# 14 dense blocks in place of 13, 23 gathered groups in place of 25, and earlier loads and verdict around the hand-over, in a graph network of two layers

## The reference, cut to what matters

```python
def _L0_gnn_ref(h, W, src, dst):      # three hops over the normalised graph
    x = h
    for _ in range(3):
        msg = (x * norm_out[:, None])[src]
        agg = segment_sum(msg, dst)
        x = 0.5 * (agg * norm_in[:, None]) + 0.5 * h
    return x @ W.T

def _L1_gnn_ref(x, edge_index, W1, b1, W2, b2, gamma, beta):
    edge_feat = concatenate([x[src], x[tgt]], axis=1)
    w = sigmoid(relu(edge_feat @ W1 + b1) @ W2 + b2)[:, 0]
    agg = segment_sum(w[:, None] * x[src], tgt)
    return layernorm(x + agg) * gamma + beta

x = layernorm(x + _L0_gnn_ref(x, ...))
x = layernorm(x + _L1_gnn_ref(x, ...))
```

## Time and profile before

| | us |
|---|---|
| median of three runs | 1170.32 (1169.7 to 1171.43) |
| the profiled execution's own time | 1174.88 |
| its span, first to last instruction | 1173.1 |
| TensorE busy | 955.8 |
| VectorE busy | 984.7 |
| ScalarE busy | 608.5 |
| POOL busy | 602.5 |

### The profile page before, as it was taken

One profiled execution on the slowest core, in us unless ns is written; L12 is line 12 of the kernel. 1 busy time (PEld: TensorE's weight loads), 2 busy tenths in 40 slices (PEclk: granted clock), 3 DMA queues, 4 the chain that ended last, 5 costly groups with the idle time before them and its releaser, 6 DMA issues.

```text
span 1173.1 us, 33827 instructions
## 1 busy us (share of the span) xinstructions
PE 955.8 (81%) x11293; PEld 789.2 (67%) x11294; DVE 984.7 (84%) x2684; ACT 608.5 (52%) x1511; POOL 602.5 (51%) x745
## 2 busy tenths in 40 slices
PE   3666666668888998989947999999999998899960
PEld 2666666657667887777825777888777777677750
DVE  7988888879999999777637999999898888788866
ACT  7555555541110000122236878788777777677765
POOL 2000000024676444466577677777777777777711
PEclk8999999979988999999968999999999999999975
DMA  3000000000000000011147677777766776676601
GB/s 98 1 0 0 0 0 0 1 1 2 2 2 3 3 3 3 20 35 43 49 128 218 194 211 217 218 213 217 222 200 207 204 209 199 191 222 198 200 15 56
DMA packets 77515, 117.43 MB, mean 100 GB/s; under 512 B 20488, under 2 KB 38972, under 8 KB 77372
## 3 DMA queue, kind: packets, MB, share of 16 engines
q1 hardware_dynamic: 58172, 63.13, 18.0%
q0 software_dynamic: 19200, 52.45, 15.9%
HBM read 108.66 MB, written 6.86 MB: 98 GB/s over the span
## 4 chain that ended last, share of the span: by engine, by line
DVE 32%; PE 26%; POOL 21%; issue 13%; ACT 4%; DMA 2%; SPq 1%; DVEq 1%; POOLq 0%; ACTq 0%
POOL region L937 13%; PE bank L1795 6%; DVE stage L1043 5%; POOL U L937 5%; PE bank L1680 5%; DVE aggT L1226 2%; PE bank L1682 2%; DVE stage L1206 2%; DVE stage L1219 2%; PE bank L1892 2%; POOL stage L937 2%; DVE aggT L1043 2%; PE bank L1917 1%; PE bank L1904 1%; PE bank L1756 1%
## 5 line engine op out<-in xcount | busy, mean ns | idle before, releaser
L937 POOL DMA_INDIRECT region<-src_split,region x272 | 265.0, 974 | 86.3 <-issue 81.5
L1795 PE MATMUL bank<-U,region 128*128 128x256 f16 (+1 forms) x1875 | 244.2, 282 | 6.6 <-DVE U L1310 3.8
L1795 PEld LDWEIGHTS bank<-U,region 128*128 128x128 fp8e4 x1875 | 184.0, 101 | 43.0 <-DVE U L1310 4.3
L2181 ACT CAST region<-bank 128x512 f16<-128x512 f32 x338 | 180.7, 591 | 0.0
L2059 ACT CAST region<-bank 128x500 f32 x202 | 119.9, 594 | 92.1 <-PE bank L1682 68.1
L2161 ACT ACTIVATE region<-bank 128x512 f16<-128x512 f32 x169 | 100.9, 597 | 63.9 <-PE bank L1895 58.3
L1680 PE MATMUL bank<-stage 128*128 128x175 f16 x544 | 92.1, 254 | 49.1 <-DVE aggT L1043 25.8
L1467 DVE SCALAR_TENSOR_TENSOR region<-bank,region 128x512 f16<-128x512 f32 x169 | 116.4, 689 | 12.8 <-ACT region L2161 9.9
L826 POOL TENSOR_TENSOR aggT<-stage 128x520 f16<-128x520 f16 x52 | 76.2, 1485 | 93.7 <-DVE stage L1203 84.1
L1892 PE MATMUL bank<-region,xs 128*128 128x256 f16 x676 | 104.2, 278 | 20.8 <-DVE region L1467 13.5
L1451 DVE TENSOR_SCALAR region<-region,stage 128x512 f16<-128x512 f16 x338 | 109.6, 366 | 12.5 <-DMA region<-slot_rows 12.5
(11 more groups left out here) (292 smaller groups left out, 2350.8 us busy)
## 6 DMA issues: line engine op xcount, KB each, us to landing
region<-slot_rows SPq DMA_DIRECT2D x169, 256.0 KB
region<-in_dst_dram SPq DMA_DIRECT2D x100, 64.0 KB
region<-src_split,region POOLq DMA_INDIRECT x272
slot_rows<-aggT SPq DMA_DIRECT2D x104, 3.2 KB
src_split<-U SPq DMA_DIRECT2D x25, 64.0 KB, 1.6
src_split<-xs SPq DMA_DIRECT2D x25, 64.0 KB, 1.5
tgt_split<-q SPq DMA_DIRECT2D x25, 64.0 KB, 1.6
region<-tgt_split SPq DMA_DIRECT2D x100, 16.0 KB
```

Of the source, the lines that this page charges most:

```text
L937: nc.gpsimd.indirect_dma_start(out=rows_of(n, i), out_offset=None, in_=src_split, in_offset=bass.IndirectOffsetOnAxis(ap=listed[n % LISTS] ...
L1795: z = nc.tensor.matmul(bank[2 * (k % 2) + p][:, 0:width], count[:, h, b * P:(b + 1) * P], U[k % 2][:, h, 0:width], start=h == 0, stop=h == ...
L2181: nc.scalar.copy(y_rows[u % 4][:, a, :], bank[3 + a][:, :]).then_inc(rows_copied, 1)
```

## The change

- `FIRST_BLOCK` goes from 12 to 11 and `POOLED` from 25 to 23: 14 dense blocks with 14 x 13 = 182 units and 28 half-blocks to sort, and 92 batches. The loop has 188 steps; the batches lie on steps 12 to 183.
- `targets_of` and `load_slots` stand further up in SP's program, and a new `first_loads` asks for list 0, the first targets and lists 1 and 2 ahead of the last `tables`. It waits for the end of the hops, the table of block 11 and the stored lists.
- `window` becomes `window_half`: two of a group's four batches per call, four DMAs, in two neighbouring batch steps; the first two windows come in steps 2 to 5, each half after a list.
- VectorE no longer waits for `pq_split` ahead of the loop, and TensorE waits in each unit of the first dense block for the two source blocks that it reads.
- `judge_landed` stands ahead of the loop, its product on TensorE after step 6 and in bank 2, `raise_flag` in step 8; TensorE's wait for the flag stands at the first `sums`.
- `qwin` and the last block of `turned_slots` have SBUF of their own.

```diff
-    POOLED = 25
+    POOLED = 23
-    FIRST_BLOCK = 12
+    FIRST_BLOCK = 11
...
-        qwin = [carve(region, taken, [2 * D], f16) for _ in range(2)]
+        qwin = [sb(f"qwin{i}", [P, 2 * D], f16) for i in range(2)]
...
-        turned_slots = [carve(aggT, taken, [P], f16) for _ in range(DENSE)]
+        turned_slots = [carve(aggT, taken, [P], f16) for _ in range(DENSE - 1)]
+        turned_slots.append(sb("turned_last", [P, P], f16))
...
+            def first_loads():
+                sp.wait_ge(hop_psum, 3 * NB)
+                sp.wait_ge(q_tabled[FIRST_BLOCK % 2], 16 * (FIRST_BLOCK // 2 + 1))
+                sp.wait_ge(slots_stored, 64 * HALF_BLOCKS)
+                load_slots(0)
+                targets_of(0)
+                load_slots(1)
+                load_slots(2)
...
             for c in range(NB + 2):
+                if c == NB + 1:
+                    first_loads()
                 tables(c, c % 2)
...
-            sp.wait_ge(hop_psum, 3 * NB)
-
-            def window(n, p):
-                if n >= 2:
-                    sp.wait_ge(ohT_ready, n - 1)
-                    sp.wait_ge(s_psum, (n - 1) * BPS)
-                first = load_four(ET.SP, base[0], n, N)
-                for q in range(BPS):
-                    sp.dma_start(qwin[p][q * QR:(q + 1) * QR, :], tgt_split[bass.ds(first[q], QR), :])\
+            window_first = [None]
+
+            def window_half(n, p, half):
+                if half == 0:
+                    if n >= 2:
+                        sp.wait_ge(ohT_ready, n - 1)
+                        sp.wait_ge(s_psum, (n - 1) * BPS)
+                    window_first[0] = load_four(ET.SP, base[0], n, N)
+                for q in range(half * BPS // 2, (half + 1) * BPS // 2):
+                    sp.dma_start(qwin[p][q * QR:(q + 1) * QR, :], tgt_split[bass.ds(window_first[0][q], QR), :])\
                       .then_inc(win_loaded[p], 16)
-                for q in range(BPS):
                     at = n * (BPS * BE) + q * BE
...
-            targets_of(0)
-            sp.wait_ge(slots_stored, 64 * HALF_BLOCKS)
-            load_slots(0)
+
             for s in range(STEPS):
                 b = batch_at[s]
-                if s + 1 < TOTAL:
+                if 2 < s + 1 < TOTAL:
                     load_slots(s + 1)
-                if s == 1:
-                    window(0, 0)
-                    window(1, 1)
-                if b is not None and b % BPS == 0 and 2 <= b // BPS + 1 < POOLED:
-                    window(b // BPS + 1, (b // BPS + 1) % 2)
+                if 2 <= s < 6:
+                    window_half((s - 2) // 2, (s - 2) // 2, s % 2)
+                if b is not None and b % BPS < 2 and 2 <= b // BPS + 1 < POOLED:
+                    window_half(b // BPS + 1, (b // BPS + 1) % 2, b % BPS)
...
-            dve.wait_ge(pq_split, NB)
             dve.wait_ge(slots_ready, HALF_BLOCKS)
...
-                if s == 0:
-                    judge_landed()
-                if s == 4:
+                if s == 8:
                     raise_flag()
...
+            judge_landed()
             first = None
             for s in range(STEPS):
...
                 pe.wait_ge(ohw_ready, b + 1)
+                if b == 0:
+                    pe.wait_ge(flag_ready, 1)
...
                 pe.wait_ge(turned_ready, u + 1)
+                if at == 0:
+                    latest = max(source_block(u, 0), source_block(u, 1))
+                    pe.wait_ge(y_split, latest + 1)
+                    pe.wait_ge(pq_split, latest + 1)
                 if u % UNITS == 0:
-                    pe.wait_ge(y_split, NB)
-                    pe.wait_ge(pq_split, NB)
                     pe.wait_ge(q_loaded[at % 2], 32 * (at // 2 + 1))
...
-                    if u == 3:
-                        pe.wait_ge(flag_ready, 1)
                     sum_pair(u - 3)
...
-                if s == 2:
+                if s == 6:
                     pe.wait_ge(chain["verdict"], 7)
-                    nc.tensor.matmul(bank[7][0:1, 0:3], one[:, :], verdict_sums[:, :], start=True, stop=True)\
+                    nc.tensor.matmul(bank[2][0:1, 0:3], one[:, :], verdict_sums[:, :], start=True, stop=True)\
```

More of the change, by code:

```diff
@@ L635, in _, with targets_of, load_slots @@
               .then_inc(w_loaded, 16)
+            def targets_of(i):
+                here = (FIRST_BLOCK + i) * P
+                if i >= 2:
+                    sp.wait_ge(pair_psum, (i - 1) * UNITS)
+                for half in range(2):
+                    sp.dma_start(q_pair[i % 2][half * HD:(half + 1) * HD, :, :],
+                                 tgt_split[here:here + P, half * D:(half + 1) * D]
+                                 .rearrange("(a r) k -> r a k", a=2)).then_inc(q_loaded[i % 2], 16)
+            def load_slots(u):
+                i, m = divmod(u, UNITS)
+                if u >= 3:
+                    sp.wait_ge(turned_ready, u - 2)
+                sp.dma_start(slots_here[u % 3][:, :], slot_rows[i, m:m + 1, :].broadcast_to([P, 8 * P]))\
+                  .then_inc(slots_loaded[u % 3], 16)
+            def first_loads():
[6 more added lines that the diff above has]
+                load_slots(2)
             def store_slots(hs):
@@ L1547, in raise_flag @@
                 dve.wait_ge(verdict_psum, 1)
-                nc.vector.tensor_copy(flag_f[:, 0:1], bank[7][0:1, 0:1])
-                nc.vector.tensor_scalar(flag_f[:, 1:2], bank[7][0:1, 1:2], float(E), None, ALU.not_equal)
-                link(nc.vector.tensor_scalar(flag_f[:, 2:3], bank[7][0:1, 2:3], 0.0, None, ALU.not_equal))
+                nc.vector.tensor_copy(flag_f[:, 0:1], bank[2][0:1, 0:1])
+                nc.vector.tensor_scalar(flag_f[:, 1:2], bank[2][0:1, 1:2], float(E), None, ALU.not_equal)
+                link(nc.vector.tensor_scalar(flag_f[:, 2:3], bank[2][0:1, 2:3], 0.0, None, ALU.not_equal))
                 link(nc.vector.tensor_tensor(flag_f[:, 0:1], flag_f[:, 0:1], flag_f[:, 1:2], ALU.add))
```

14 lines of the change are left out of this document (removed).

## The result

The changed kernel takes **1194.0 us** (median, 1190.56 to 1195.39), the kernel before in the same comparison 1170.41: 23.6 us slower by the medians. The ratio over all executions is 1.0189, interval 1.0171 to 1.0207, some 22 us. The prediction said 1169.8 with a range of 1159 to 1178. The profiled execution took 1194.06 us, its span is 1192.2 (1173.1 before).

The account below looks back on a forecast made before the run. POOL's gathers were taken to bound the loop's last 288 us, the engines' unit steps the part before. Terms -1.0 + 10.5 - 5.2 - 4.8 = -0.5 us took 1170.3 to 1169.8 us; range 1159 to 1178.

Parts of the forecast that it names:

- Term 2: Hops: two more half-blocks to sort cost +10.5 us: 3.8, 4.9 and 1.8 us in first, second and third hop.
- The upper end: Hops: all work of the two added half-blocks, blocked operations included, in a row: 14.3 us.
- Terms 3 and 4: After the hops: first list usable earlier, -5.2 us; list 3 ahead of window halves in first steps, -4.8 us.
- rival D: Hand-over: SP or its queue still held by tables and slot stores, first list no earlier, 1175.0 us; chance 0.08.
- Its stated sign: Hand-over: first list more than 4 us after VectorE's last hop operation would show the early request failing.
- rival C: First steps: lists stay behind the windows on SP, the 4.8 us are lost again, 1174.6 us; chance 0.15.
- term 1: Loop: gathers leave the path, unit steps set the pace, 484.1 us against 485.1, so -1.0 us.
- rival E: Loop: gathers still bind it, having 4% of room only; some 5 us more, 1175 us; chance 0.05.
- the ends that were given: Loop: 14.6 us less if added steps cost 2.32 us; 17 more if POOL-paced steps returned for a third.
- The tail: Final stage: 25 blocks in seven groups as before, so 0.
- Rival B: Hops: sorting finds room, 4.2 us instead of 10.5, 1163.5 us, or no price, 1159.3 us; chance 0.27.
- The stated test: Hops: the last hop's end 10 us later if right, less than 6 us later if wrong.

Follow-up runs that it names:

- The spacing alone: Kernel before, 26 half-blocks, with only the starts of the sorting set to the changed kernel's gaps of 2, 2, 3: 1201.14 us, ratio 1.0244.
- the passes spread: Numbers three steps after the scan, not two, on two buffers: changed kernel 1160.65 us; kernel before with 26 half-blocks at gaps 2, 2, 3: 1166.51 us.
- The mix alone: Kernel before with 14 dense blocks and 23 groups; lists, target slices and verdict as they were: 1199.7 us, ratio 1.0222.
- the hand-over edits alone: Changed kernel with its early lists, target halves and early verdict, but 12 dense blocks and 25 groups as before: 1173.49 us, ratio 1.000.
- the scan first: Changed kernel with two buffers of running sums and the scan first in VectorE's step instead of last, numbers still two steps after: 1180.01 us, ratio 1.0068.

## Why the prediction was wrong

**Term 2, the sorting, is the step that failed: +10.5 predicted, +38.1 measured.** It counted how many scans, numberings and places come to each hop, and priced them by VectorE's time and its gaps. `sorted_at` was read for these counts only, and where in the steps the passes fall was put at nothing. The same line also says that with 28 starts three passes fall into one step nine times, which the kernel before had nowhere. The upper end, 14.3 us, called "everything in a row", was no bound: it took for granted that an engine that is busy 96% of a stretch stays busy when passes move. The spacing alone, with no pass added, took 28.2 us. Its cost is shown as waiting of the two engines for each other in the second hop; how it comes about in the third is open.

The price of the half-blocks themselves came out near +10.5, but by chance as far as the runs show. Two half-blocks more at the same gaps cost 11.0 us with the passes spread (598.02 for 587.06) and 9.9 without (633.43 for 623.58). Both times this lies in the third hop, where the two begin: 131.9 for 120.0 us, and 139.5 for 129.8. The prediction had put 8.7 of its 10.5 us into the first two hops and 1.8 into the third, because neither engine is full there. No run adds a half-block to the first or the second hop at equal gaps, so those two parts are not tested. Against the kernel before, 28 half-blocks with the passes spread cost 2.7 us (598.02 for 595.34). A hand-over of 35.1 for 43.4, a loop of 477.9 for 485.1 and a tail of 46.5 for 49.3 more than make up for that: the span of that kernel, 1157.4, is 15.7 us shorter than before (12.4 by the medians).

On the blocked operations: of the 25 of line 1286 in the second hop 9 take over 0.5 us; before, it was 10 of 25 (line 1277 there). By the rule of the Trainium skill (SBUF — State Buffer, section Who interferes with whom) four more of POOL's products were estimated at 6 us of blocked VectorE; the blocking is there (1076 ns at most, 293 ns as a rule), but on this line it didn't grow with the half-blocks.

```profile
L1286 DVE TENSOR_TENSOR U<-t,U x25: 291/293/1076, 380.5 to 485.4; 128x128 f16<-128x128 f32 x25
```

**Terms 3 and 4, the hand-over and the first steps: -10.0 predicted, -9.1 measured.** The first list is used 5.9 us after the hops' last operation, 5.3 predicted and 10.4 before, so rival D is out. Its stated sign, more than 4 us, is met all the same; it was set too low, since the forecast itself stood at 5.3. Of rival C something is left: VectorE's idle times for the first lists are 0.2 to 1.8 us, 4.3 us in six places, where the fourth list alone cost 6.22. The total is near in part by luck, since 2.3 of the 9.1 us came with the mix, which the terms did not count; the edits gave 6.8 of the 10.0. What the text didn't say is that these terms hang on term 1: with POOL as the pace, the same edits gave 0 (1173.49 beside 1173.07).

**Term 1, the loop: -1.0 predicted, -7.2 measured.** The mechanism holds: no waits for gathered rows, the gathers' last start (1117.1) 28 us ahead of the last unit, rival E out. The sizes were a little high. 91 intervals with a batch took 3.034 us each instead of 3.095, 81 without 2.491 instead of 2.50: 5.6 + 0.7 = 6.3 us. The measured value lies within the ends that were given (-14.6 to +17).

**The tail: 0 predicted, -2.7 measured.** The mix alone has it too (45.5 us for 49.3), the hand-over edits alone don't (49.4). Its cause was not looked into.

**The range** failed with term 2. Rival B (sorting finds room) was the only one on the hops, and it was on the wrong side: the loss came out larger than the forecast, not smaller. No rival asked for the price of the steps' arrangement, though its sign was open. The stated test did tell: the hops' end was to come 10 us later and came 38 later.

## What to carry to other kernels

When work is spread over the steps of a loop by a formula, list what each step gets before and after a change of the count, and look for steps in which passes meet that had been apart; a sum of durations over the stretch can't see it. Here two engines that feed each other and were both nearly full lost time with uneven steps: TensorE can be two steps ahead at most, and a count that waits for a scan holds up the products queued behind it. A second buffer that lets a pass be moved by one step was worth some 33 us (1194.0 to 1160.65). And an edit that starts a stage sooner is to be priced together with what paces the stage: the same edits gave 0 with POOL as the pace and 6.8 us without.

## What the runs showed of the hardware

Short pauses of TensorE showed in its clock. In the step above it had no work from 396.09 to 398.75, 2.66 us. The mean granted clock of the next two stretches, 6.4 us of work, was 0.76 and 0.72 of 2.4 GHz, and 1.00 again in the third (us, busy with count, clock, DMA share, GB/s). Both means are mixtures of the two levels: from 400.00 to 403.42 the clock was at 0.50, 1.2 GHz (last row).

```profile
396.09:398.75 2.66, 0.00 (x0) 1.00 0.00 0
398.75:401.13 2.38, 2.38 (x21) 0.76 0.00 0
401.13:405.15 4.02, 4.02 (x27) 0.72 0.02 3
405.19:408.05 2.86, 2.86 (x26) 1.00 0.02 6
...
400.00:403.42 3.42, 3.42 (x23) 0.50 0.02 3
```

The 25 products from 401.13 on took 4.02 us, the 25 from 405.19 on 2.93, so this pause cost over 1 us more than its own length, just where VectorE waited for the first 12 of them. The clock falls to 0.50 in the same way in the next two periods of this hop (from 430.7 and from 461.4); with the scan first or the passes apart it stays at 1.00 in the period shown. The Trainium skill (TensorE: Matmul & The Clock Gate, section A second HAM failure mode: psum-queue depth-cycling) tells of a kernel whose TensorE idles briefly between groups of matmuls and pays for it in clock; the trace agrees, with a pause for another engine's result in the place of a cycling queue.
